# Merging triangular inverses of a gated delta rule: 64x64 tiles on the diagonal in place of 128x128 matmuls

## The chip, the cores and the metric

The kernel runs on one core of one Trainium2 chip. The metric is the device time of one execution in microseconds (us), the median of three runs. A core has a matmul engine (PE, with its weight loads shown apart as PEld), a vector engine (DVE), an activation engine (ACT), a general engine (POOL) and an engine that issues transfers (SP).

## The reference

The program is a decoder of two layers with attention, cross-attention and feed-forward parts. The change lies in the attention part of the second layer, a delta rule with gates. Per token t, for 16 sequences (B), 8 heads (H), 256 tokens, keys of 64 (DK) and values of 128 (DV):

```python
def step(carry, inp):
    ...
    s = s * alpha[..., None]
    u = jnp.einsum('bhd,bhdv->bhv', kt, s)
    s = s - beta[..., None] * jnp.einsum('bhd,bhv->bhdv', kt, u)
    s = s + beta[..., None] * jnp.einsum('bhd,bhv->bhdv', kt, vt)
    out = jnp.einsum('bhdv,bhd->bhv', s, qt)
```

The kernel doesn't step through the tokens. It forms for each tile of 128 tokens the lower triangular matrix of decayed products of keys and solves with its inverse: (I + L)^-1 applied to the values, and from that the outputs.

## The kernel before

The function is `delta_stage`, called once. The work is 32 "duos" (DUOS) of 2 units each (u = 0, 1). A unit is 2 heads h with 2 tiles s of 128 tokens, so it has TAU = 4 square matrices k of 128 x 128. Everything is fp32; a matmul in the program then shows in the trace as 2 weight loads and 2 matmul records.

`schedule` writes the order for every engine alike, and each engine runs its own instructions in that order:

```python
for m in range(DUOS + LATE):
    for slot in range(10):
        if LATE <= m:
            third(m - LATE, slot)
        if m < DUOS:
            first(m, slot)
        if 1 <= m <= DUOS:
            second(m - 1, slot)
            lanes(m - 1, slot)
```

So a round m works on three duos at once. There are 35 rounds of 10 slots. In words:

- `first` on PE: slot 0 scores the diagonal (L2930), and slots 1, 3, 5, 7, 9 score levels 0 to 4 (`level`, L2915), each as tiles of 64 rows x 128 columns of the array. DVE cuts the results into AB (L3081, L3092), and POOL multiplies the decays into `src` (L2899 once per unit after the diagonal, L2880 to L2890 after each level). Level 0 waits for both the decay (`decayed`) and the cut of the diagonal; level v waits for the scaling and the cut of level v - 1.
- `second`, one round later: level 5 in slot 2, level 6 in slot 6, the products between the two tiles in slot 8 (L2969). ACT cuts levels 5 and 6 (L3173, L3181) and scales `src` between them (L3159, L3162).
- `lanes` on DVE: the inverses of the 16 x 16 blocks, one lane per block, step by step. SP moves blocks out and in through DRAM: AB to l_img to lane_l, lane_x and lane_t to x_img and xt_img, and those as whole matrices to X and XT.
- `third`, three rounds later: slots 0 to 5 merge the 16 x 16 inverses to 32, to 64 and to 128. X holds the inverse, XT its transpose, LT is the triangle. Slot 0 forms y4 = LT'X (L2989), which DVE masks into Y4 (L3127). Slot 1 forms XT's and X's new blocks (L2997, L2999), which DVE subtracts (L3134, L3136). Slot 2 forms y5 (L3005), which ACT copies to Y5 (L3203). Slot 3 forms the new blocks (L3011, L3013); ACT writes XT (L3210), DVE X (L3141). Slot 4 forms y6 (L3019), ACT copies it to Y6 (L3215). Slot 5 forms XT's last block (L3025), ACT writes it (L3218). Slots 6 to 9 solve and make the outputs (L3033 to L3057).

Between the slots 4 and 5 of `third` no other PE work stands; between any two others stands a level, the diagonal or the cross product. Every merge matmul before uses all 128 rows and 128 columns of the array (weights 128 x 128), with 64 or 32 moving columns.

Of the kernel before, what the change touches and what calls it, by code (L numbers as in the profile page):

```python
# [21 lines left out]
P = 128  # L22
# [2617 lines left out]
def delta_stage(nc, name, ident, unit_in, unit_v, unit_o):  # L2640
# [27 lines left out]
    with Stage(nc, name) as st:  # L2668
# [17 lines left out]
        real = st.sb("real", [P, LOW + 1, P // 2])  # L2686
        keys_mask = st.sb("keys_mask", [P, LOW, 2, P // 2], I32)
# [54 lines left out]

        def rows_cols(k):
            h, s = divmod(k, 2)
            return slice(h * DK, (h + 1) * DK), slice(s * P, (s + 1) * P)
# [23 lines left out]
        with st.block() as block:  # L2769
            @block.sync  # L2770
            def _(sp):
                sp.wait_ge(zeroed, 1)
                for s in range(2):
                    sp.dma_start(whole(x_img, s), X[:, 0, :, :, :].rearrange("p u k t -> p (u k) t")).then_inc(img_zeroed, 16)
                    sp.dma_start(whole(xt_img, s), X[:, 0, :, :, :].rearrange("p u k t -> p (u k) t")).then_inc(img_zeroed, 16)
# [27 lines left out]
                def lanes_out(n):  # L2803

                    sp.wait_ge(lanes_done, n + 1)
                    if n < 2:
                        sp.wait_ge(img_zeroed, 64)
                    else:
                        sp.wait_ge(x_loaded[n % 2], 32 * (n // 2))
# [36 lines left out]
            def _(pool):  # L2846
                pool.memset(X[:, 0, :, :, :], 0.0).then_inc(zeroed, 1)
# [15 lines left out]
                pool.memset(Y5[:, :, :, :], 0.0).then_inc(zeroed, 1)  # L2863
                pool.memset(Y6[:, :, :, :], 0.0).then_inc(zeroed, 1)
# [42 lines left out]
            def _(pe):  # L2907
                pe.wait_ge(zeroed, 6)
                pe.wait_ge(masks_cast, 4)

                def level(n, v, u):
                    for k in (0, 2, 1, 3):
                        h, s = divmod(k, 2)
                        rows, cols = rows_cols(k)
                        ins = pe.matmul(lb[u][:, h, :, s * 64:(s + 1) * 64].rearrange("p a (b i) -> p a b i", i=1 << v),  # L2915
                                        src[rows, n % 3, u, 3, cols],
                                        halves(src[rows, n % 3, u, 0:2, cols], v)[:, :, :, 1, :], start=True, stop=True)
                    return ins
# [54 lines left out]
                def third(n, slot):  # L2973
                    w = n % 2
                    for u in range(2):
                        LT = lambda k: AB[:, n % KEPT, u, k // 2, 0, k % 2, :]
                        y = wp[u][:, :, :].rearrange("p k t -> p (k t)")[:, 0:256].rearrange("p (k t) -> p k t", k=TAU)
                        d = dp[u][:, :, :].rearrange("p k t -> p (k t)")
                        d1 = d[:, 0:256].rearrange("p (k t) -> p k t", k=TAU)
                        d2 = d[:, 256:512].rearrange("p (k t) -> p k t", k=TAU)  # L2980
                        if slot == 0:
                            if u == 0:
                                pe.wait_ge(x_loaded[w], 32 * (n // 2 + 1))
# [4 lines left out]
                            for k in range(TAU):  # L2988
                                ins = pe.matmul(y[:, k, :].rearrange("p (b i) -> p b i", i=16), LT(k),  # L2989
                                                halves(X[:, w, u, :, :], 4)[:, k, :, 0, :], start=True, stop=True)  # L2990
                            ins.then_inc(y4_scored, 1)
                        elif slot == 1:
# [3 lines left out]
                            for k in range(TAU):  # L2996
                                pe.matmul(d1[:, k, :].rearrange("p (b i) -> p b i", i=16), Y4[:, u, k, :],  # L2997
                                          halves(XT[:, w, u, :, :], 4)[:, k, :, 1, :], start=True, stop=True)
                                ins = pe.matmul(d2[:, k, :].rearrange("p (b i) -> p b i", i=16), XT[:, w, u, k, :],  # L2999
                                                halves(Y4[:, u, :, :], 4)[:, k, :, 0, :], start=True, stop=True)  # L3000
                            ins.then_inc(x4_scored, 1)
                        elif slot == 2:
                            pe.wait_ge(x4_ready, after(n, u))
                            for k in range(TAU):
                                ins = pe.matmul(y[:, k, :].rearrange("p (b i) -> p b i", i=32), LT(k),  # L3005
                                                halves(X[:, w, u, :, :], 5)[:, k, :, 0, :], start=True, stop=True)
                            ins.then_inc(y5_scored, 1)
                        elif slot == 3:
                            pe.wait_ge(y5_ready, after(n, u))
                            for k in range(TAU):  # L3010
                                pe.matmul(d1[:, k, :].rearrange("p (b i) -> p b i", i=32), Y5[:, u, k, :],  # L3011
                                          halves(XT[:, w, u, :, :], 5)[:, k, :, 1, :], start=True, stop=True)
                                ins = pe.matmul(wp[u][:, 2, k * 32:(k + 1) * 32], XT[:, w, u, k, :], Y5[:, u, k, 0:32],  # L3013
                                                start=True, stop=True)
                            ins.then_inc(x5_scored, 1)
                        elif slot == 4:
                            pe.wait_ge(x5_ready, after(n, u))
                            for k in range(TAU):
                                ins = pe.matmul(y[:, k, :], LT(k), X[:, w, u, k, 0:64], start=True, stop=True)  # L3019
                            ins.then_inc(y6_scored, 1)  # L3020
                        elif slot == 5:
                            pe.wait_ge(y6_ready, after(n, u))
                            pe.wait_ge(xt5_ready, after(n, u))
                            for k in range(TAU):
                                ins = pe.matmul(d1[:, k, :], Y6[:, u, k, :], XT[:, w, u, k, 64:128],  # L3025
# [37 lines left out]
            def _(dve):  # L3063
# [5 lines left out]
                dve.wait_ge(zeroed, 6)  # L3069
# [3 lines left out]
                dve.wait_ge(masks_cast, 4)  # L3073
# [44 lines left out]
                def third(n, slot):  # L3118
                    w = n % 2
                    for u in range(2):  # L3120
                        y = wp[u][:, :, :].rearrange("p k t -> p (k t)")[:, 0:256].rearrange("p (k t) -> p k t", k=TAU)
                        d = dp[u][:, :, :].rearrange("p k t -> p (k t)")
                        d1 = d[:, 0:256].rearrange("p (k t) -> p k t", k=TAU)
                        d2 = d[:, 256:512].rearrange("p (k t) -> p k t", k=TAU)
                        if slot == 0:
# [3 lines left out]
                                              real[:, LOW, :].rearrange("p (b i) -> p b i", i=16).unsqueeze(1)  # L3129
                                              .to_broadcast([P, TAU, 4, 16]), ALU.mult).then_inc(y4_ready, 1)  # L3130
                        elif slot == 1:
                            dve.wait_ge(x4_scored, after(n, u))
                            xt = halves(XT[:, w, u, :, :], 4)[:, :, :, 1, :]
                            dve.tensor_tensor(xt, xt, d1.rearrange("p k (b i) -> p k b i", i=16), ALU.subtract)  # L3134
# [3 lines left out]
                        elif slot == 3:  # L3138
                            dve.wait_ge(x5_scored, after(n, u))
                            x = X[:, w, u, :, 0:32]  # L3140
                            dve.tensor_tensor(x, x, wp[u][:, 2, :].rearrange("p (k j) -> p k j", k=TAU), ALU.subtract).then_inc(x5_ready, 1)  # L3141
# [7 lines left out]
            def _(act):  # L3149
# [44 lines left out]
                def third(n, slot):  # L3194
                    w = n % 2
                    for u in range(2):
                        y = wp[u][:, :, :].rearrange("p k t -> p (k t)")[:, 0:256].rearrange("p (k t) -> p k t", k=TAU)
                        d1 = dp[u][:, :, :].rearrange("p k t -> p (k t)")[:, 0:256].rearrange("p (k t) -> p k t", k=TAU)
                        if slot == 2:
                            act.wait_ge(y5_scored, after(n, u))  # L3200
                            for b in range(2):
                                rows = slice(b * 64 + 32, b * 64 + 64)
                                ins = act.activation(Y5[rows, u, :, b * 64:b * 64 + 32], y[rows, :, b * 32:b * 32 + 32],  # L3203
                                                     ACT.Copy)
                            ins.then_inc(y5_ready, 1)
                        elif slot == 3:
                            act.wait_ge(x5_scored, after(n, u))
                            for b in range(2):
                                rows = slice(b * 64, b * 64 + 32)
                                ins = act.activation(XT[rows, w, u, :, b * 64 + 32:b * 64 + 64],  # L3210
                                                     d1[rows, :, b * 32:b * 32 + 32], ACT.Copy, scale=-1.0)
                            ins.then_inc(xt5_ready, 1)
                        elif slot == 4:
                            act.wait_ge(y6_scored, after(n, u))
                            act.activation(Y6[64:128, u, :, 0:64], y[64:128, :, :], ACT.Copy).then_inc(y6_ready, 1)  # L3215
                        elif slot == 5:
                            act.wait_ge(xt6_scored, after(n, u))
                            act.activation(XT[0:64, w, u, :, 64:128], d1[0:64, :, :], ACT.Copy, scale=-1.0  # L3218
# [290 lines left out]
```

## Time and profile before

| | |
|---|---|
| median of 3 runs | 7280.35 us (7275.85 to 7287.11) |
| profiled execution | 7309.51 us, its span 7307.6 us |
| busy in the span | PE 5607.2, DVE 4967.0, ACT 3317.2, PEld 3111.2, POOL 2010.7 us |
| delta stage on PE | from 3910.4 to 5036 us |

The time is that of the whole program; the stage that is changed is about 1,126 us of it. PE's clock is granted at one of two levels, full (2.4 GHz) or half (1.2 GHz), shown as 1.00 or 0.50 of full speed; a value between is the mean of a stretch. A matmul's record begins when it enters the array and is pipelined with the next, so intervals between starts say more than the length of a record.

### The profile page before, as it was taken

How to read it: one execution, taken by the hardware profiler on the slowest of the kernel's cores; microseconds unless marked ns; L12 is line 12 of the kernel's file. 1: busy time of each engine (PE TensorE's matmuls, PEld its weight loads, DVE VectorE, ACT ScalarE, POOL GpSimd, SP SyncE). 2: the span in 40 equal slices, each digit the busy share in tenths (PEclk: the TensorE clock that was granted, in tenths of full speed). 3: DMA queues.
4: the chain of work that ended last, by engine and by line, in shares of the span. 5: the costliest groups of instructions: out<-in, count | busy, mean ns of one | idle time of the engine just before them, and what ended most of it. 6: DMA issues, size and time to landing. Idle time of an engine off the chain costs nothing. (4 is left out here: it accounts for less than half of the span.)

```text
span 7307.6 us, 135138 instructions
## 1 busy us (share of the span) xinstructions
PE 5607.2 (77%) x43987; PEld 3111.2 (43%) x43987; DVE 4967.0 (68%) x8964; ACT 3317.2 (45%) x4792; POOL 2010.7 (28%) x2592
## 2 busy tenths in 40 slices
PE   3786647688888839950787999997666699999759
PEld 1343435222222224420555999996534333333334
DVE  5564663799999944457896666663544599999654
ACT  0233424466666712220783444443223377777512
POOL 1101324566766720000004555551313200000000
PEclk6898878799999969975997999897787799999979
DMA  2220016222222210000233434342204422222200
GB/s 59 49 44 9 6 31 211 76 56 58 56 58 57 50 37 10 0 2 3 115 125 115 122 110 126 107 117 64 75 6 158 133 66 64 63 65 65 60 11 12
DMA packets 756225, 484.32 MB, mean 66 GB/s; under 512 B 484248, under 2 KB 682753, under 8 KB 754369
## 3 DMA queue, kind: packets, MB, share of 16 engines
q1 hardware_dynamic: 755904, 480.05, 23.2%
q8 instruction: 202, 3.31, 0.2%
q14 instruction: 119, 0.97, 0.0%
HBM read 282.34 MB, written 196.37 MB: 66 GB/s over the span
## 5 line engine op out<-in xcount | busy, mean ns | idle before, releaser
L1481 ACT ACTIVATE c0a_raised<-c0a_sb 128x1024 f32<-128x1024 f32 (+1 forms) x832 | 837.3, 1025 | 320.5 <-PE c0a_sb L1293 316.2
L1246 POOL TENSOR_SCALAR c0a_prob<-c0a_raised 128x1024 f32<-128x1024 f32 (+1 forms) x832 | 866.1, 1041 | 395.1 <-ACT c0a_raised L1481 363.5
L1481 ACT ACTIVATE c1a_prob<-c1a_sb 128x1024 f32<-128x1024 f32 (+1 forms) x832 | 828.9, 1029 | 205.6 <-PE c1a_sb L1293 202.0
L1369 DVE TENSOR_REDUCE c0a_pmax<-c0a_sa 128x2 f32<-128x802 f32 (+1 forms) x704 | 697.2, 990 | 86.3 <-PE c0a_sa L1261 81.9
L1369 DVE TENSOR_REDUCE c1a_pmax<-c1a_sa 128x2 f32<-128x802 f32 (+1 forms) x704 | 698.3, 992 | 70.7 <-PE c1a_sa L1261 66.7
L1261 PE MATMUL c0a_sa<-c0a_K,c0a_Q 48*128 48x401 bf16 (+1 forms) x2048 | 479.4, 354 | 196.8 <-DVE c0a_pmax L1369 101.5
L1261 PE MATMUL c1a_sa<-c1a_K,c1a_Q 48*128 48x401 bf16 (+1 forms) x2048 | 466.2, 346 | 103.4 <-DVE c1a_pmax L1369 47.7
L1312 PE MATMUL c0a_pv<-c0a_prob,c0a_V 128*9 128x256 f32 x6656 | 533.9, 392 | 4.8 <-POOL c0a_prob L1246 4.1
L1312 PE MATMUL c1a_pv<-c1a_prob,c1a_V 128*9 128x256 f32 x6656 | 519.4, 383 | 0.7 <-issue 0.5
L1261 PEld LDWEIGHTS c0a_sa<-c0a_K,c0a_Q 48*128 48x128 bf16 x2048 | 131.1, 94 | 688.6 <-DVE c0a_pmax L1369 330.9
L3092 DVE COPY_PREDICATED dd_AB<-dd_keys_mask,dd_lb 128x512 f32<-128x512 int32 x320 | 286.7, 959 | 156.2 <-PE dd_lb L2915 142.2
L1293 PE MATMUL c0a_sb<-c0a_Q,c0a_K 51*128 51x256 bf16 (+1 forms) x3328 | 384.1, 279 | 0.8 <-ACT c0a_raised L1481 0.8
L1293 PE MATMUL c1a_sb<-c1a_Q,c1a_K 51*128 51x256 bf16 (+1 forms) x3328 | 376.6, 272 | 0.9 <-ACT c1a_prob L1481 0.9
L1374 DVE TENSOR_REDUCE c0a_pmax<-c0a_sa 128x1 f32<-128x401 f32 (+1 forms) x640 | 361.5, 565 | 12.8 <-PE c0a_sa L1261 10.4
L1374 DVE TENSOR_REDUCE c1a_pmax<-c1a_sa 128x1 f32<-128x401 f32 (+1 forms) x640 | 362.8, 567 | 5.1 <-PE c1a_sa L1261 2.0
L1261 PEld LDWEIGHTS c1a_sa<-c1a_K,c1a_Q 48*128 48x128 bf16 x2048 | 127.6, 93 | 555.4 <-DVE c1a_pmax L1369 276.3
L2880 POOL TENSOR_TENSOR dd_src<-dd_src,dd_total 128x128 f32<-128x128 f32 x512 | 219.3, 450 | 395.4 <-PE dd_lb L2915 395.2
L1537 POOL TENSOR_TENSOR c1o_yn<-c1o_y,c1o_r 128x256 f32<-128x256 f32 x8 | 6.1, 782 | 1146.4 <-DMA c1o_r<-y_scale 1146.4
L2915 PE MATMUL dd_lb<-dd_src 64*128 64x128 f32 x3584 | 310.6, 319 | 10.1 <-POOL dd_total L2884 4.9
L2915 PEld LDWEIGHTS dd_lb<-dd_src 64*128 64x128 f32 x3584 | 260.3, 217 | 38.4 <-issue 9.2
L2538 PE MATMUL dp_qk<-d_HT,dp_wk 128*128 (+1 forms) x128 | 43.4, 421 | 284.5 <-DVE dp_bmat L2597 213.1
L930 DVE TENSOR_REDUCE s_pmax<-s_sa 128x2 f32<-128x512 f32 x256 | 170.5, 687 | 125.4 <-PE s_sa L822 123.1
(595 smaller groups left out, 12068.0 us busy)
## 6 DMA issues: line engine op xcount, KB each, us to landing
unit_in<-dp_res SPq DMA_DIRECT2D x64, 512.0 KB, 2.6
dd_src<-unit_in SPq DMA_DIRECT2D x64, 512.0 KB, 6.3
k_ctx<-c0k_parts SPq DMA_DIRECT2D x16, 1200.8 KB, 4.7
c0a_K<-k_ctx SPq DMA_DIRECT2D x128, 150.1 KB
k_ctx<-c1k_parts SPq DMA_DIRECT2D x16, 1200.8 KB, 4.7
c1a_K<-k_ctx SPq DMA_DIRECT2D x128, 150.1 KB
unit_v<-dp_vs SPq DMA_DIRECT2D x64, 256.0 KB, 2.8
dd_l_img<-dd_AB SPq DMA_DIRECT2D x64, 256.0 KB
```

The lines of the kernel that those rows point to most:

```text
L930: dve.tensor_reduce(pmax[:, u, 2 * h + tiles[0]:2 * h + tiles[0] + m, k:k + 1] .rearrange("p m a -> p (m a)"), sa[:, i % 2, 0:m * (b - a)] ...
L1246: pool.tensor_scalar(prob[0:r, in_ring(v, c), :, :, :], raised[0:r, in_ring(v, c), :, :, :], 1.0, math.exp(-FLOOR), ALU.min, ALU.max).then ...
L1261: return pe.matmul(tile[:, 0:b - a], Q[at, v, pr, s * P:(s + 1) * P], K[at, v, pr, a:b], start=True, stop=True)
L1293: ins = pe.matmul(sb_[0:r, in_both(v, c), e, pr, :], K[at, v, pr, c * P:c * P + r], Q[at, v, pr, :], start=True, stop=True)
L1312: ins = pe.matmul(pv[x * 32:x * 32 + V9, 0, :], V[0:r, v, c, x, :], prob[0:r, in_ring(v, c), x // 2, x % 2, :], start=(c == 0), stop=(c == ...
L1369: dve.tensor_reduce(pmax[:, u, :, 2 * pr + s, k], sa2[:, :, 0:w], AX.X, ALU.max).then_inc(a_reduced, 1)
L1374: dve.tensor_reduce(pmax[:, u, x % 2, 2 * pr + s, k:k + 1], sa1[:, 0:w], AX.X, ALU.max).then_inc(a_reduced, 1)
L1481: act.activation(dst[0:r, in_ring(v, c), :, :, :], sb_[0:r, in_both(v, c), :, :, :], ACT.Exp).then_inc(b_exp, 1)
L2538: pe.matmul(qk[:, u, 0, :], wk[:, rows], x, start=True, stop=True)
L2880: pool.tensor_tensor(kq[:, x], kq[:, x], tot[:, :, 0].unsqueeze(2).to_broadcast([P, nb, c]), ALU.mult)
L2915: ins = pe.matmul(lb[u][:, h, :, s * 64:(s + 1) * 64].rearrange("p a (b i) -> p a b i", i=1 << v), src[rows, n % 3, u, 3, cols], halves(sr ...
L3092: dve.copy_predicated(out[:, :, :, 1, :], mask.unsqueeze(1).to_broadcast([P, 4, P // c, c]), lb[u][:, :, :, 0:P].rearrange("p h a (b i) -> ...
```

## The change

Blocks of 16, 32 and 64 never cross the middle of the 128 x 128 matrix, so the merges are done on its two diagonal quarters:

- X is kept as the two diagonal blocks of 64 x 64, one under the other in [128, 64]. Y4 and Y6 halve to 64 columns, Y5 quarters to 32.
- Slots 0, 1 and 2 issue two matmuls (b = 0, 1) with weights of 64 x 64 and 32 moving columns for each old one of 128 x 128 with 64. The two use the array's quarters at rows and columns 0 to 63 and 64 to 127.
- Slot 3 issues for each k two matmuls with weights of 64 rows x 32 columns and one with 64 x 64, in turn.
- Slots 4 and 5 keep the number of matmuls; each uses one 64 x 64 quarter.
- Level 6 of `second` loads 64 columns of weights in place of 128.
- DVE: Y4 and X halve in elements; XT of slot 1 becomes two operations of 64 partitions; X of slot 3 is 32 partitions. A new pair_mask [128, 32] is made once at the start.
- ACT: Y5 is one operation of 128 x 128 in place of two of 32 x 128.
- SP: X is loaded by two transfers of 64 partitions in place of one, so each duo waits for 48 and not 32.
- At the start: two memsets of POOL (Y5, Y6) are gone, Y4's halves.

```diff
-        X = st.sb("X", [P, 2, 2, TAU, P])
-        Y4 = st.sb("Y4", [P, 2, TAU, P])
-        Y5 = st.sb("Y5", [P, 2, TAU, P])
-        Y6 = st.sb("Y6", [P, 2, TAU, P])
+        X = st.sb("X", [P, 2, 2, TAU, P // 2])
+        Y4 = st.sb("Y4", [P, 2, TAU, P // 2])
+        Y5 = st.sb("Y5", [P, 2, TAU, P // 4])
+        Y6 = st.sb("Y6", [P, 2, TAU, P // 2])
...
+        def half(b):
+
+            return slice(b * 64, (b + 1) * 64)
...
-                    sp.dma_start(X[:, n % 2, :, :, :].rearrange("p u k t -> p (u k) t"), whole(x_img, n % 2)
-                                 ).then_inc(x_loaded[n % 2], 16)
+                    for b in range(2):
+                        sp.dma_start(X[half(b), n % 2, :, :, :].rearrange("p u k t -> p (u k) t"),
+                                     whole(x_img, n % 2)[half(b), :, half(b)]).then_inc(x_loaded[n % 2], 16)
...
                 def level(n, v, u):
+                    keys = 64 if v == 6 else P
...
-                                        src[rows, n % 3, u, 3, cols],
+                                        src[rows, n % 3, u, 3, s * P:s * P + keys],
...
                         if slot == 0:
...
                             for k in range(TAU):
-                                ins = pe.matmul(y[:, k, :].rearrange("p (b i) -> p b i", i=16), LT(k),
-                                                halves(X[:, w, u, :, :], 4)[:, k, :, 0, :], start=True, stop=True)
+                                for b in range(2):
+                                    ins = pe.matmul(y[half(b), k, :].rearrange("p (b i) -> p b i", i=16),
+                                                    LT(k, half(b), half(b)),
+                                                    halves(X[half(b), w, u, :, :], 4)[:, k, :, 0, :],
+                                                    start=True, stop=True)
...
                         elif slot == 3:
                             pe.wait_ge(y5_ready, after(n, u))
                             for k in range(TAU):
-                                pe.matmul(d1[:, k, :].rearrange("p (b i) -> p b i", i=32), Y5[:, u, k, :],
-                                          halves(XT[:, w, u, :, :], 5)[:, k, :, 1, :], start=True, stop=True)
-                                ins = pe.matmul(wp[u][:, 2, k * 32:(k + 1) * 32], XT[:, w, u, k, :], Y5[:, u, k, 0:32],
-                                                start=True, stop=True)
+                                for b in range(2):
+                                    pe.matmul(d1[b * 64:b * 64 + 32, k, :], Y5[half(b), u, k, :],
+                                              XT[half(b), w, u, k, b * 64 + 32:b * 64 + 64], start=True, stop=True)
+                                ins = pe.matmul(wp[u][0:64, 2, k * 32:(k + 1) * 32], XT[0:64, w, u, k, 0:64],
+                                                Y5[0:64, u, k, :], start=True, stop=True)
                             ins.then_inc(x5_scored, 1)
                         elif slot == 4:
                             pe.wait_ge(x5_ready, after(n, u))
                             for k in range(TAU):
-                                ins = pe.matmul(y[:, k, :], LT(k), X[:, w, u, k, 0:64], start=True, stop=True)
+                                ins = pe.matmul(y6[64:128, k, :], LT(k, half(0), half(1)), X[0:64, w, u, k, :],
+                                                start=True, stop=True)
```

How PE's instructions stand before, from slot 0 of a round to the level of slot 3; each row is a line, what it writes and reads, the partitions x free size of the result, and how many in a row:

```order
-L2989 MATMUL dd_wp<-dd_X,dd_AB 128x64 x8
-L2930 MATMUL dd_lb<-dd_src 128x128 x8
-L2997 MATMUL dd_dp<-dd_XT,dd_Y 128x64
-L2999 MATMUL dd_dp<-dd_Y,dd_XT 128x64
...
-L2915 MATMUL dd_lb<-dd_src 128x2x64 x8
-L3005 MATMUL dd_wp<-dd_X,dd_AB 128x64 x8
-L2915 MATMUL dd_lb<-dd_src 128x2x64 x8
-L3011 MATMUL dd_dp<-dd_XT,dd_Y 128x64
-L3013 MATMUL dd_wp<-dd_Y,dd_XT 128x32
...
-L3019 MATMUL dd_wp<-dd_X,dd_AB 128x64 x8
-L3025 MATMUL dd_dp<-dd_XT,dd_Y 128x64 x8
```

The pairs of lines 2997 and 2999, and of 3011 and 3013, come 8 times each. The same place with the change, whose lines have moved down by 9 to 21:

```order
+L3000 MATMUL dd_wp<-dd_X,dd_AB 64x32 x16
+L2940 MATMUL dd_lb<-dd_src 128x128 x8
+L3011 MATMUL dd_dp<-dd_XT,dd_Y 64x32 x2
+L3015 MATMUL dd_dp<-dd_Y,dd_XT 64x32 x2
...
+L2924 MATMUL dd_lb<-dd_src 128x2x64 x8
+L3024 MATMUL dd_wp<-dd_X,dd_AB 64x32 x16
+L2924 MATMUL dd_lb<-dd_src 128x2x64 x8
+L3031 MATMUL dd_dp<-dd_XT,dd_Y 32x32 x2
+L3033 MATMUL dd_wp<-dd_Y,dd_XT 64x32
...
+L3039 MATMUL dd_wp<-dd_X,dd_AB 64x64 x8
+L3046 MATMUL dd_dp<-dd_XT,dd_Y 64x64 x8
```

No instruction has moved past another; the merges' matmuls of a round have gone from 64 to 104, and in slot 3 a pair with 32 result partitions and a single one with 64 now stand in turn, 8 times.

DVE in slot 1, before and with the change (one unit after the other):

```order
-L3134 TENSOR_TENSOR dd_XT<-dd_XT,dd_dp 128x16x16
-L3136 TENSOR_TENSOR dd_X<-dd_X,dd_dp 128x16x16
-L3134 TENSOR_TENSOR dd_XT<-dd_XT,dd_dp 128x16x16
-L3136 TENSOR_TENSOR dd_X<-dd_X,dd_dp 128x16x16
...
+L3157 TENSOR_TENSOR dd_XT<-dd_XT,dd_dp 64x4x2x16 x2
+L3160 TENSOR_TENSOR dd_X<-dd_X,dd_dp 128x8x16
+L3157 TENSOR_TENSOR dd_XT<-dd_XT,dd_dp 64x4x2x16 x2
+L3160 TENSOR_TENSOR dd_X<-dd_X,dd_dp 128x8x16
```

DVE has one operation more per unit here, and the elements of each partition that X's takes are half.

## Rows read from the trace of the kernel before

**Rows 1.** Busy time by engine in three stretches of the delta stage.
```profile
core 0: us, PE busy (x) PEld busy (x) DVE busy (x) ACT busy (x) POOL busy (x), PEclk, DMA share, GB/s
3910.40:3977.10 66.70, 51.09 (x384) 41.03 (x384) 49.42 (x98) 15.39 (x48) 53.20 (x128) 0.61 0.29 84
3977.10:4926.90 949.80, 949.80 (x8751) 885.03 (x8752) 620.02 (x1487) 391.39 (x1176) 511.81 (x1237) 0.91 0.40 116
4926.90:5036.00 109.10, 107.99 (x856) 102.97 (x852) 40.41 (x112) 40.54 (x120) 18.34 (x45) 0.86 0.25 68
```

**Rows 2.** DVE's groups, 3977.10 to 4926.90 us: busy us, mean ns, idle before.
```profile
L3092 DVE COPY_PREDICATED dd_AB<-dd_keys_mask,dd_lb 128x512 f32<-128x512 int32 x281 | 251.0, 960 | 135.7 <-PE dd_lb L2915 126.7 <-DMA dd_l_img<-dd_AB 7.3
L3081 DVE COPY_PREDICATED dd_AB<-dd_eye_mask,dd_lb 128x512 f32<-128x512 int32 x56 | 37.9, 732 | 8.4 <-PE dd_lb L2930 8.4
```

**Rows 3.** Waits, 3982 to 4960 us: waited for in total, times, longest.
```profile
POOL dd_src L2880 <- PE dd_lb L2915: 449.4, 144, 5.9
ACT dd_Y L3203 <- PE dd_wp L3005: 282.3, 58, 9.8
PEld dd_dp L3053 <- issue: 9.6, 29, 0.3
```

**Rows 4.** Busy time in two neighbouring stretches of different clock, columns as in Rows 1.
```profile
4430.40:4444.00 13.60, 13.60 (x80) 12.81 (x80) 7.40 (x19) 5.60 (x20) 6.13 (x16) 0.50 0.01 2
4444.00:4498.60 54.60, 54.60 (x550) 50.74 (x548) 36.68 (x89) 22.33 (x65) 30.35 (x72) 1.00 0.50 144
```

**Rows 5.** PE in order of time at full clock, slots 3 to 5: start, length, records.
```profile
4395.51 0.43 PE L3011 MATMUL dd_dp<-dd_XT,dd_Y 128*128 128x64 f32 x2
...
4399.20 1.18 PE L2915 MATMUL dd_lb<-dd_src 64*128 64x128 f32 x16
4400.31 2.00 PE L3019 MATMUL dd_wp<-dd_X,dd_AB 128*128 128x64 f32 x16
...
4404.03 1.16 PE L2915 MATMUL dd_lb<-dd_src 64*128 64x128 f32 x16
```

**Rows 6.** PE in order of time, the next round's slot 8 to slot 3.
```profile
4410.57 1.14 PE L2969 MATMUL dd_lb<-dd_src 64*128 64x256 f32 x8
4411.63 0.49 PE L3053 MATMUL dd_dp<-dd_W,dd_AB 128*128 128x128 f32 x2
...
4415.60 2.00 PE L2989 MATMUL dd_wp<-dd_X,dd_AB 128*128 128x64 f32 x16
4417.53 1.16 PE L2930 MATMUL dd_lb<-dd_src 64*128 64x128 f32 x16
4418.62 0.43 PE L2997 MATMUL dd_dp<-dd_XT,dd_Y 128*128 128x64 f32 x2
...
4422.33 1.18 PE L2915 MATMUL dd_lb<-dd_src 64*128 64x128 f32 x16
4423.45 2.00 PE L3005 MATMUL dd_wp<-dd_X,dd_AB 128*128 128x64 f32 x16
```

**Rows 7.** Weight loads by shape: rows*columns, busy us, mean ns.
```profile
L2989 PEld LDWEIGHTS dd_wp<-dd_X,dd_AB 128*128 128x128 f32 x512 | 59.6, 191 | 3.6
L859 PEld LDWEIGHTS s_pv<-s_prob,s_VG 128*32 128x32 f32 x1024 | 20.3, 108 | 45.4 <-issue 20.4 <-DVE s_osb L981 12.8 <-ACT s_prob L1075 12.1
```

**Rows 8.** Busy time inside one level's matmuls, columns as in Rows 1.
```profile
4404.10:4404.84 0.74, 0.74 (x14) 0.74 (x16) 0.05 (x1) 0.72 (x3) 0.01 (x1) 1.00 0.00 0
```

**Rows 9.** POOL in order of time, the decay of one round.
```profile
4418.37 2.51 POOL L2899 TENSOR_TENSOR dd_src<-dd_src 128x512 f32<-128x512 f32 x2
```

**Rows 10.** ACT in order of time around slot 4.
```profile
4399.88 0.82 ACT L3159 ACTIVATE dd_src<-dd_src,dd_total 128x64 f32<-128x64 f32 x3
4400.61 0.73 ACT L3162 ACTIVATE dd_src<-dd_src,dd_total 128x32 f32<-128x32 f32 x3
4401.45 0.38 ACT L3215 ACTIVATE dd_Y<-dd_wp 64x256 f32<-64x256 f32 x1
```

**Rows 11.** POOL in order of time at the stage's start.
```profile
3907.56 0.95 POOL L2863 MEMSET dd_Y<- 128x1024 f32 x1
3908.45 1.23 POOL L2864 MEMSET dd_Y<- 128x1024 f32 x1
```

More of the change, by code:

```diff
@@ L2686, in delta_stage @@
         real = st.sb("real", [P, LOW + 1, P // 2])
+        pair_mask = st.sb("pair_mask", [P, P // 4])
         keys_mask = st.sb("keys_mask", [P, LOW, 2, P // 2], I32)
@@ L2996, in third @@
                             for k in range(TAU):
[L2997 to L3000, printed above, removed]
+                                for b in range(2):
+                                    pe.matmul(d1[half(b), k, :].rearrange("p (b i) -> p b i", i=16), Y4[half(b), u, k, :],
+                                              halves(XT[half(b), w, u, :, half(b)], 4)[:, k, :, 1, :],
+                                              start=True, stop=True)
+                                for b in range(2):
+                                    ins = pe.matmul(d2[half(b), k, :].rearrange("p (b i) -> p b i", i=16),
+                                                    XT[half(b), w, u, k, half(b)],
+                                                    halves(Y4[half(b), u, :, :], 4)[:, k, :, 0, :],
+                                                    start=True, stop=True)
                             ins.then_inc(x4_scored, 1)
@@ L3004, in third @@
                             for k in range(TAU):
-                                ins = pe.matmul(y[:, k, :].rearrange("p (b i) -> p b i", i=32), LT(k),
-                                                halves(X[:, w, u, :, :], 5)[:, k, :, 0, :], start=True, stop=True)
+                                for b in range(2):
+                                    ins = pe.matmul(y[half(b), k, :], LT(k, half(b), half(b)), X[half(b), w, u, k, 0:32],
+                                                    start=True, stop=True)
                             ins.then_inc(y5_scored, 1)
@@ L3068, in _ @@
                                 ident[:, :].unsqueeze(1).to_broadcast([P, TAU, P])).then_inc(masks_cast, 1)
-                dve.wait_ge(zeroed, 6)
+                dve.tensor_tensor(pair_mask[:, :], real[:, LOW, 0:P // 4], real[:, LOW, P // 4:P // 2], ALU.add
+                                  ).then_inc(masks_cast, 1)
+                dve.wait_ge(zeroed, 4)
                 for s in range(2):
@@ L3128, in third @@
                                               y.rearrange("p k (b i) -> p k b i", i=16),
-                                              real[:, LOW, :].rearrange("p (b i) -> p b i", i=16).unsqueeze(1)
-                                              .to_broadcast([P, TAU, 4, 16]), ALU.mult).then_inc(y4_ready, 1)
+                                              pair_mask[:, :].rearrange("p (b i) -> p b i", i=16).unsqueeze(1)
+                                              .to_broadcast([P, TAU, 2, 16]), ALU.mult).then_inc(y4_ready, 1)
                         elif slot == 1:
                             dve.wait_ge(x4_scored, after(n, u))
-                            xt = halves(XT[:, w, u, :, :], 4)[:, :, :, 1, :]
-                            dve.tensor_tensor(xt, xt, d1.rearrange("p k (b i) -> p k b i", i=16), ALU.subtract)
+                            for b in range(2):
+                                xt = halves(XT[half(b), w, u, :, half(b)], 4)[:, :, :, 1, :]
+                                dve.tensor_tensor(xt, xt, d1[half(b), :, :].rearrange("p k (b i) -> p k b i", i=16),
+                                                  ALU.subtract)
                             x = halves(X[:, w, u, :, :], 4)[:, :, :, 0, :]
```

67 lines of the change are left out of this document (33 added, 34 removed).

## The prediction

> **What bounds the kernel now.** I read first the busy time by stretch, since the change touches one stage only. In its long middle stretch of 949.80 us PE is busy for all 949.80 us, DVE for 620.02, POOL for 511.81 and ACT for 391.39 [rows 1]. The diagonal's cut runs twice a round and 56 times there [rows 2], so the stretch is 28 rounds and a round takes 33.92 us; of that DVE is busy for 22.1, POOL for 18.3 and ACT for 14.0. The list of waits says the same from the other side: POOL and ACT wait for PE's results for hundreds of us, and what PE itself waited for is some 10 us of issue [rows 3]. So PE bounds the stage; what its order and its clock cost is what the change can give back.
>
> Two things hide in a "busy" PE. One is the clock. There are 8751 / 28 = 312.5 matmul records a round [rows 1]; at full clock 550 records take 54.60 us, 0.0993 us each, and at half clock 80 take 13.60 [rows 4]. A round at full clock would thus take 31.0 us, and the stage pays 2.9 us a round for stretches at half clock. The other is what a matmul costs. In slots 4 and 5, 32 records go in 3.72 us (4400.31 to 4404.03), and slot 1's 32 records in 3.71 (4418.62 to 4422.33) [rows 5, 6]. That is 0.112 us a record, whether 64 or, in slot 3 (4395.51 to 4399.20, 3.69 us), in part 32 columns stream. So the matmul's moving side doesn't set the price, the load of 128 weight columns does. Levels, whose weights have 64 rows on either half of the array, give 14 records in 0.74 us, 0.053 each [rows 8]: two loads go beside each other. Slots 0 to 5 of the merges cost before 1.93 + 3.71 + 1.93 + 3.69 + 3.72 = 15.0 us a round [rows 5, 6] (slot 2 is like slot 0).
>
> **The change, part by part.**
>
> Price of a record on a quarter. No row has a load of 64 fp32 columns. A load record of 128 columns lasts 191 ns, one of 32 lasts 108 [rows 7]: linear between them, 64 columns last 136. I take the step between starts to be proportional to columns, 0.112 x 64/128 = 0.056 us; the bounds are 0.028 (that of 32 columns, were only moving columns to count) and 0.112 (nothing gained). Two quarters with their own rows and columns I take to run beside each other, as the levels' halves do.
>
> Price of a change of tile size. Slot 0's step is 1.93 us with 16 x 0.112 = 1.79 in it, 0.14 over; a level is 1.09 to 1.11 us with 16 x 0.053 = 0.85 in it, 0.25 over [rows 5, 6]. The mean is 0.19 us a change, about 0.1 of which is the first weight load that nothing hides; with 64 columns that part halves, so 0.13 us. Bounds are 0 and 0.19.
>
> The slots then are, at full clock: slot 0, 32 records in pairs, 16 x 0.056 + 0.13 = 1.0; slot 1, 64 records, 1.9; slot 2, 1.0; slots 4 and 5, 32 records on one quarter one after the other, 1.8 + 0.13 = 1.9. Slot 3 has 8 groups. In each the two 32-column matmuls go beside each other and the 64-column one behind them: 2 x 0.03 + 2 x 0.056 = 0.17 us, 1.4 together. But 64x32 and 64x64 stand in turn, so the tile size changes 16 times more: 16 x 0.13 = 2.1, together 3.5 us (from 1.4 + 0.13 without a price on the turn to 1.4 + 16 x 0.19 = 4.4). The sum is 9.3 in place of 15.0: 5.7 us less a round, a round of 25.3 us at full clock.
>
> The Trainium skill, page "TensorEngine Tiling (Array Packing)", Key Properties, states that a change of tiling mode drains TensorE, and this speaks against slot 3. The trace agrees that a change costs something: 0.25 us over at a level. By the page slot 3 pays in all 16 changes, which is what my sum takes; without it the round would be 23.3 us.
>
> Level 6. Half the weight columns, but 128 moving columns stay. The cross product streams 256 columns in 8 records in 1.06 us (4410.57 to the next at 4411.63) [rows 6]: less 0.2 for the change, 0.107 a record with pairs beside each other, 0.213 each for 256 columns. So 128 columns are 0.107 each for themselves, and nothing is gained. Bound: 0 to 0.4 us.
>
> What is late next. As PE's slots shrink, two waits show that PE now covers.
> First, level 0 in slot 1 waits for POOL's decay of both units, which ends at 4418.37 + 2.51 = 4420.88, 5.3 us after slot 0 began at 4415.60 [rows 6, 9]. POOL starts it behind the last scaling of the round before, so it doesn't move. PE would be at level 0 after 1.0 + 1.1 + 1.9 = 4.0 us: up to 1.3 us of wait, less half a level since unit 0 may start first. I take 1.0. Behind PE queue slots 2 and 3, and nobody else is late.
> Second, slot 5 waits for ACT's Y6 with no level between. Before, ACT first ran the scaling of level 5 up to 4401.34 and then Y6 at 4401.45, 1.1 us after slot 4 began, while PE had 1.8 us of slot 4 to do [rows 5, 10]. Slot 4 now takes 0.9 us, so PE stands at slot 5 after 1.0, while unit 0's Y6 is ready at some 1.6 and unit 1's 0.38 later. I take 0.8 (0.5 to 1.2).
> DVE has 22 us of work a round, its slot 1 grows by one operation a unit and slots 0 and 1 lose elements: about even. It keeps under PE's 27. So a round at full clock is 25.3 + 1.8 = 27.1 us. SP's third transfer a duo lies rounds ahead of its use: nothing.
>
> The clock. The half-clock stretch shown begins at 4430.40 [rows 4], where slot 3 of its round ends (slot 2 begins at 4423.45, slot 3 some 3 us later [rows 6]); there the array streams the fewest columns. Such a stretch of 13.6 us loses 6.8, so 2.9 us a round is one in 2.3 rounds. The stretches of slow feeding become shorter in slots 0 to 2, but slot 3 stays a weak one and the two waits add gaps. I can't derive this; between 0 and the 2.9 us of now I take 1.2. A round: **28.3 us**, 5.6 less than 33.9.
>
> The sum. 28 rounds and the one from 4926.90 on: 29 x 5.6 = 163 us. The last three rounds have merges and no levels; of the 109.10 us from there 75 are theirs [rows 1], and each loses its merges' 5: 15. The start: two memsets of POOL, 0.89 + 1.2 us, stand ahead of PE's first matmul [rows 11]; DVE has a mask more to make there; I take 1.2 us (0 to 2.2). Together 179. The profiled execution took 7309.51 us, so 7130 for one like it, which lies 29.2 above the median of the runs; against the median **7101 us**.
>
> **The rivals.**
>
> B: the turn of sizes in slot 3 is free. If a 64x32 matmul and a 64x64 one follow each other without a drain, slot 3 is 1.5 us, the round 25.1 with its waits and 26.2 with clock: 29 x 7.7 + 16 = 240, **7040 us**. For it: the price 0.19 was seen only between work of different shapes with a wait on a semaphore at the boundary. Against it: from L2915 to L3019 0.25 us is paid, and the list of waits has no such wait of PE [rows 3, 5].
>
> C: a record has a least price of its own. Then 64 columns cost no less than the best rate seen, and 208 records (104 matmuls) stand where 128 stood. Nothing in the program goes faster than the 0.053 us a record of the levels [rows 8], so the trace can't exclude that this is a floor. With 0.053 the merges are 11.0 + 1.2 of the changes of before + 2.1 = 14.3, a gain of 0.7; the case decides for slower from 0.056 on. At 0.068, a level's 1.09 us over its 16 records, it is 14.1 (its change within) + 2.1 = 16.2, 1.2 us more a round: 32 x 1.2 less 1, **7320 us**, and with 0.053 it is 7257. Against it: two levels' records go in pairs, so the issue isn't what spaces them.
> The Trainium skill, "TensorE: Matmul & The Clock Gate", Wait — 56ns, not 53.3ns?, gives about 62 ns per MATMUL where hardware decode is off, and 25 ns otherwise. By the first this case comes out, with an estimate of 208 x 0.062 + 3.3 = 16.2 us for the merges; the 0.053 of the trace speaks for the second.
>
> D: the clock stays low. If thinner feeding keeps PE at half clock for a share h of the time, the round is 25.3 / (1 - h/2), the waits gone. Break-even is h = 0.51; now it is 2 x 2.9 / 33.9 = 0.17. For h = 0.6 it is 36.1 us and the time **7345**. For it: the first three rounds, which have no merges and in which PE is busy for 51 of 66.7 us, ran at a mean of 0.61 [rows 1]. Against it: the merges' quarters still stream in nearly all of the time.
>
> E: another engine sets the pace. Cuts of 0.96 us [rows 2] stand twice between two levels, and DVE does the merges' own steps first; with each slot only 2 to 3 us long, some end late, and 27.1 becomes 30.5 with no further cost of clock: 29 x 3.4 + 16 = 115, **7166 us**.
>
> **How the numbers follow.** I give my forecast 0.5, B 0.16, C 0.16, D 0.08, E 0.10. The likeliest is 7101 us; its own range, from the bounds of slot 3 (±1 us), waits (±0.5) and clock (±1.2), is 7055 to 7150. The range takes in B's 7040 with its bounds and E, from 7015 to 7225; beyond it are most of C and D and a rest of B. What a measurement can tell from no change is 0.2%, 15 us. Faster: A, B, E and a part of C, 0.80; within 0.2%: 0.06 from C; slower: 0.14 from C and D.
>
> **What would show it.** In order of time at full clock: slot 0 about 1.0 us from its first merge record to the diagonal's, slot 1 1.9, slots 4 and 5 together 1.9 and a gap between them ahead of which ACT's Y6 stands; slot 3 3.5 us (1.5 would be B, over 4.4 a drain dearer than seen). Ahead of level 0 PE idles about 1 us behind POOL's L2899, now a later line. If the intervals between records on quarters are 0.053 or more even in pairs, it is C. The mean clock of the middle stretch is to be at or above 0.93; under 0.75 it is D. A round with DVE busy at over 0.9 is E. The forecast is wrong if quarters' weight loads don't run beside each other, since slots 0 to 2 then save nothing.

## The result and the profile after

The changed kernel takes 7201.78 us (7196.43 to 7213.07, 4 runs), the one before 7283.73 (4 runs): a ratio of 0.9894 (0.9878 to 0.9909), some 82 us faster. I had forecast 7101 and 179 us. The time is within the stated range of 7015 to 7225; the gain is less than half of the 179 us.

The profiled execution has a span of 7211.4 us. Two stretches of the delta stage, the 28 full rounds and the tail, that answer to [rows 1] (busy us and records by engine, then the clock):

```profile
core 0: us, PE busy (x) PEld busy (x) DVE busy (x) ACT busy (x) POOL busy (x), PEclk, DMA share, GB/s
3956.66:4846.96 890.30, 861.62 (x10978) 761.35 (x10980) 634.57 (x1543) 376.12 (x1120) 508.87 (x1231) 0.82 0.40 115
4846.96:4945.00 98.04, 94.61 (x1168) 85.06 (x1168) 41.53 (x121) 38.05 (x111) 19.74 (x50) 0.74 0.27 74
```

A round takes 31.8 us (890.30 / 28) where it took 33.9. PE now idles for 28.7 us in all, 1.0 a round, and its mean clock has gone from 0.91 to 0.82. The stage as a whole (3889.95 to 4945.00) went from 1126 to 1055 us, some 70 less: 59 in the full rounds, 11 in the tail, nothing in the first three rounds (66.7 us in both). The two profiled spans differ by 96 us, since the stage also starts 20 us earlier. That part isn't the change: in the profile of b_wide3 below, which alters nothing ahead of slot 3, the full rounds begin at 3952.38, 25 us earlier than before too.

PE in order of time, which answers to [rows 5, 6] (start, length, records; in brackets how long PE sat idle before, and what ended it):

```profile
4401.43 1.12 PE L3000 MATMUL dd_wp<-dd_X,dd_AB 64*64 64x32 f32 x32
4402.48 1.16 PE L2940 MATMUL dd_lb<-dd_src 64*128 64x128 f32 x16
4403.57 0.30 PE L3011 MATMUL dd_dp<-dd_XT,dd_Y 64*64 64x32 f32 x4
...
4405.55 0.72 PE L2924 MATMUL dd_lb<-dd_src 64*128 64x128 f32 x8
4406.76 0.72 PE L2924 MATMUL dd_lb<-dd_src 64*128 64x128 f32 x8 [0.48 <-POOL dd_src L2907]
4407.41 1.12 PE L3024 MATMUL dd_wp<-dd_X,dd_AB 64*64 64x32 f32 x32
4408.64 0.71 PE L2924 MATMUL dd_lb<-dd_src 64*128 64x128 f32 x8
4409.80 0.72 PE L2924 MATMUL dd_lb<-dd_src 64*128 64x128 f32 x8 [0.45 <-DVE dd_AB L3115]
4410.45 0.25 PE L3031 MATMUL dd_dp<-dd_XT,dd_Y 64*32 64x32 f32 x4
4410.63 0.30 PE L3033 MATMUL dd_wp<-dd_Y,dd_XT 64*64 64x32 f32 x2
4410.86 0.25 PE L3031 MATMUL dd_dp<-dd_XT,dd_Y 64*32 64x32 f32 x4
...
4414.06 2.08 PE L2924 MATMUL dd_lb<-dd_src 64*128 64x128 f32 x16
4416.06 1.86 PE L3039 MATMUL dd_wp<-dd_X,dd_AB 64*64 64x64 f32 x15
```

The slots did shrink: slot 0 is 1.05 us (4401.43 to 4402.48), slot 1 1.98, a group of slot 3 0.41 (4410.45 to 4410.86). Level 0 waits for POOL's decay, level 5 (the next two rows of L2924) for a cut of DVE. But the 16 records of L2924 from 4414.06 last 2.08 us, where the 16 of L2940 at 4402.48 last 1.16: the clock has halved. Three neighbouring stretches of the same round, to be held against [rows 4]:

```profile
4402.00:4412.90 10.90, 9.87 (x200) 8.49 (x196) 8.86 (x24) 2.59 (x8) 8.11 (x18) 1.00 0.67 184
4412.90:4423.10 10.20, 10.20 (x85) 9.37 (x84) 6.25 (x15) 5.16 (x19) 5.37 (x14) 0.51 0.28 103
4423.10:4444.00 20.90, 19.87 (x309) 17.28 (x308) 16.34 (x41) 8.18 (x22) 12.81 (x31) 0.99 0.40 93
```

The clock falls between 1.5 and 3.4 us after slot 3's first record, and slot 3 takes 3.28 us. Half-clock stretches now come 28 times in 28 rounds and last 317 us together. Before they came 13 times, 178 us, each 3.8 to 4.1 us after slot 3's first record, so just behind its 3.69 us. No round of the changed kernel is free of them, so its full-clock round is an estimate: 26.2 us, the full-clock round of the grouped kernel below, and the 1.38 that slot 3 is longer here give 27.6. The kernel with wider streams, also below, gives the same: its full-clock rounds take 28.2 us, 0.62 of which slot 3 is longer there. So the clock costs 4.2 us a round. That is where most of the expected gain went.

### The profile page after: what moved, and what is told of

The parts are those of the page before. It is cut to its first block and busy times, and to the rows that moved or that the text cites. A ratio compares the mean times of both kernels' runs of the same rounds, so it can differ in the third digit from the quotient of the medians.

```text
span 7211.4 us, 140243 instructions
## 1 busy us (share of the span) xinstructions
PE 5480.0 (76%) x46501; PEld 2956.1 (41%) x46547; DVE 4981.5 (69%) x9029; ACT 3299.7 (46%) x4728; POOL 2005.8 (28%) x2590
## 5 line engine op out<-in xcount | busy, mean ns | idle before, releaser
L1369 DVE TENSOR_REDUCE c1a_pmax<-c1a_sa 128x2 f32<-128x802 f32 (+1 forms) x704 | 698.1, 992 | 70.7 <-PE c1a_sa L1261 66.7
L2924 PE MATMUL dd_lb<-dd_src 64*128 64x128 f32 (+1 forms) x3584 | 359.3, 347 | 39.0 <-POOL dd_src L2907 15.9
L2924 PEld LDWEIGHTS dd_lb<-dd_src 64*128 64x128 f32 (+1 forms) x3584 | 292.8, 230 | 79.6 <-issue 28.5
```

The lines of the kernel that those rows point to most:

```text
L1369: dve.tensor_reduce(pmax[:, u, :, 2 * pr + s, k], sa2[:, :, 0:w], AX.X, ALU.max).then_inc(a_reduced, 1)
L2924: ins = pe.matmul(lb[u][0:keys, h, :, s * 64:(s + 1) * 64] .rearrange("p a (b i) -> p a b i", i=1 << v), src[rows, n % 3, u, 3, s * P:s * ...
```

## The experiments

Each ratio is to runs of the kernel before on the same chip (medians 7274 to 7284 us); two variants are best compared by their ratios. Full-clock rounds are medians of the rounds without a half-clock stretch. Theory 1: the clock falls where the array is fed with few columns, and slot 3, thin and with sixteen changes of tile size, is the place. Theory 2: it goes by how much of the array is in use, so quarter tiles lower it whatever streams. Beside them, rivals for the waits.

**Before, slot 3 with wider streams.**

```diff
-    pe.matmul(d1[:, k, :].rearrange("p (b i) -> p b i", i=32), Y5[:, u, k, :],
-              halves(XT[:, w, u, :, :], 5)[:, k, :, 1, :], start=True, stop=True)
-    ins = pe.matmul(wp[u][:, 2, k * 32:(k + 1) * 32], XT[:, w, u, k, :], Y5[:, u, k, 0:32],
-                    start=True, stop=True)
+    pe.matmul(dp[u][:, k, :], Y5[:, u, k, :], XT[:, w, u, k, :], start=True, stop=True)
+    ins = pe.matmul(wp[u][:, 2 + k // 2, k % 2 * 64:k % 2 * 64 + 64], XT[:, w, u, k, :],
+                    Y5[:, u, k, 0:64], start=True, stop=True)
```

DVE and ACT read the same elements from their new places.

> The kernel before with one thing changed: slot 3 streams more columns through the same weights (128 in place of 64 for the transposed block, 64 in place of 32 for the other); the results that are used are the same. Theory 1 (the half-clock stretch comes where the array is fed with few columns per time): slot 3 keeps its 3.7 us, since 128 weight columns bound it, the stretches of half clock after it go, a round falls from 34.0 to 31.0 us, the mean clock of the stage rises from 0.91 to near 1.00 and the program is 80 to 90 us faster (about 7195). Theory 2 (the clock has to do with something else, such as the small tiles of the levels or the waits of the other engines): no change within 15 us.

Measured: 7185.8 us, ratio 0.9885 (0.9861 to 0.991). The 28 rounds, in the columns of [rows 1], and slot 3 in order of time:

```profile
3952.38:4820.38 868.00, 868.00 (x8746) 807.11 (x8748) 626.78 (x1487) 389.52 (x1176) 510.20 (x1235) 1.00 0.44 127
```
```profile
4394.94 0.49 PE L3011 MATMUL dd_dp<-dd_XT,dd_Y 128*128 128x128 f32 x2
4395.27 0.33 PE L3012 MATMUL dd_wp<-dd_Y,dd_XT 128*128 128x64 f32 x2
...
4398.66 1.18 PE L2915 MATMUL dd_lb<-dd_src 64*128 64x128 f32 x16
```

Slot 3 lasts 3.72 us as before (3.69 in [rows 5]), with the same instructions and twice the columns, and no half-clock stretch is left: 31.0 us a round, the number that [rows 1, 4] give for full clock. Theory 1 is shown for the kernel before: with all else equal, the columns of slot 3 decide whether the clock falls. It is also a gain of 88 us, as much as the whole change brought.

**After, slot 3 all of 64x32 tiles.**

```diff
-    ins = pe.matmul(wp[u][0:64, 2, k * 32:(k + 1) * 32], XT[0:64, w, u, k, 0:64],
+    ins = pe.matmul(wp[u][32:64, 2, k * 32:(k + 1) * 32], XT[0:64, w, u, k, 32:64],
```

> The changed kernel with slot 3 all of one tile size: the matmul with weights 64x64 uses only the 32 columns whose results are read, so all 24 matmuls are 64x32 and the 16 changes of size inside slot 3 are gone. If a change of size drains the array at about 0.13 us, slot 3 falls from 3.3 to about 1.5 us at full clock. Theory 1 (thin feeding sets off the half clock): also the low stretch of each round gets rarer, as slot 3 was the thinnest place: a round from 31.9 to between 25.5 and 29, the program 7040 to 7140 us. Theory 2 (the clock goes by how much of the array is in use): the low stretch stays in each round, a round 30.2, 7145 to 7155 us. If turns are free: no change.

Measured: 7055.35 us, ratio 0.9708 (0.9683 to 0.9733).

```profile
3950.40:4706.40 756.00, 697.21 (x10978) 618.28 (x10978) 632.10 (x1541) 372.71 (x1120) 508.52 (x1231) 0.94 0.47 135
```
```profile
4390.30 0.22 PE L3031 MATMUL dd_dp<-dd_XT,dd_Y 64*32 64x32 f32 x2
...
4390.93 1.18 PE L2924 MATMUL dd_lb<-dd_src 64*128 64x128 f32 x16
4392.04 1.14 PE L3039 MATMUL dd_wp<-dd_X,dd_AB 64*64 64x64 f32 x16
4394.25 1.14 PE L3046 MATMUL dd_dp<-dd_XT,dd_Y 64*64 64x64 f32 x16 [1.07 <-ACT dd_Y L3235]
```

A round is 27.0 us, 25.6 at full clock. Slot 3 is 0.63 us from its first record at 4390.30 to the level, shorter than I thought possible, and PE hits the next wait: 1.07 us for ACT's Y6 ahead of slot 5. Low stretches still come 22 times, but short, 88 us in all. They begin 4.4 to 5.9 us after slot 3's first record, so no longer in slot 3 but behind this wait (slot 5 begins 3.95 us after it).

**After, slot 3 grouped.**

```diff
     for k in range(TAU):
         for b in range(2):
             pe.matmul(d1[b * 64:b * 64 + 32, k, :], ...
+    for k in range(TAU):
         ins = pe.matmul(wp[u][0:64, 2, ...
```

> The changed kernel with the order inside slot 3 changed: for a unit first the eight 64x32 matmuls, then the four 64x64 ones, so 4 changes of size a round inside slot 3 in place of 16; same matmuls. With a price of about 0.13 us a change slot 3 goes from 3.3 to 1.8 us at full clock; if changes are free it stays. The clock may stay as low as it is; 7130 to 7160 us if it does, less if the low stretch gets rarer.

Measured: 7053.78 us, ratio 0.9697 (0.967 to 0.9724).

```profile
3970.28:4711.48 741.20, 704.01 (x10972) 621.68 (x10972) 622.48 (x1541) 372.80 (x1120) 505.15 (x1230) 0.99 0.48 138
```
```profile
4405.10 0.44 PE L3031 MATMUL dd_dp<-dd_XT,dd_Y 64*32 64x32 f32 x16
4405.47 0.65 PE L3034 MATMUL dd_wp<-dd_Y,dd_XT 64*64 64x32 f32 x8
4406.05 0.44 PE L3031 MATMUL dd_dp<-dd_XT,dd_Y 64*32 64x32 f32 x16
4406.42 0.65 PE L3034 MATMUL dd_wp<-dd_Y,dd_XT 64*64 64x32 f32 x8
4407.00 1.18 PE L2924 MATMUL dd_lb<-dd_src 64*128 64x128 f32 x16
```

The same matmuls in another order: slot 3 at full clock is 1.90 us (4405.10 to 4407.00) where it was 3.28 (8 groups of 0.41) with twelve changes of size more, 0.115 us a change. And the clock falls in 2 rounds where it fell in all 28, though the tiles, the columns and the two waits ahead of slot 3 (0.47 and 0.44 us, 0.48 and 0.45 in the changed kernel) are the same. This rules out theory 2, that quarter tiles lower the clock whatever streams. It also sharpens theory 1: the number of columns is the same too, and what is shorter is the time that they are spread over. The sum is 5.3 us a round, of which 1.4 is slot 3 itself and some 3.9 the clock.

**After, wider streams in slots 0 to 3.** Each 32 moving columns become 64, e.g.

```diff
-    ins = pe.matmul(y[half(b), k, :], LT(k, half(b), half(b)), X[half(b), w, u, k, 0:32],
+    ins = pe.matmul(y6[half(b), k, :], LT(k, half(b), half(b)), X[half(b), w, u, k, :],
```

> The changed kernel with 64 moving columns in place of 32 in every merge matmul of slots 0 to 3 (in slot 3's single matmul the same 32 columns twice); the extra results are not read. Weights and tile sizes as in the changed kernel. Theory 1 (feeding): PE's slots 0 to 2 keep their length within 0.1 us, the half-clock stretch of each round gets shorter or rarer, a round falls from 31.9 to 27 to 30 us and the program is at 7060 to 7150 us. Theory 2 (share of the array in use): no change, 7200, or slower by what the columns cost, up to 1 us a round (7230).

Measured: 7167.71 us, ratio 0.9856 (0.9831 to 0.9881).

```profile
3968.85:4807.95 839.10, 806.20 (x10972) 687.48 (x10974) 627.20 (x1540) 374.69 (x1120) 507.21 (x1231) 0.92 0.42 122
```

30.0 us a round and 11 low stretches in place of 28. The streams cost 0.03 us in slot 0, but slot 3 goes from 3.28 to 3.90. I take the reason to be that a 32-column weight load doesn't hide 64 moving columns; nothing tests it by itself. I had left that out of the forecast, and the time lies above my 7060 to 7150 for theory 1, though below the 7200 of theory 2.

**After, level 6 with 128 weight columns again,** on the grouped kernel:

```diff
-    keys = 64 if v == 6 else P
+    keys = P
```

> The kernel with slot 3 grouped, and level 6 with 128 weight columns as before the change. Its 128 moving columns bound it either way, so I expect no change: 7054 us within 10.

Measured: 7059.89 us, ratio 0.9689 (0.9663 to 0.9714); the grouped kernel's 0.9697 (0.967 to 0.9724) doesn't differ. Rounds at full clock are 26.3 us against 26.2. This part of the change brings at most 0.1 us a round.

**Grouped, POOL's last scaling of unit 1 behind the decay.**

```diff
-                        for u in range(2):
+                        for u in range(1 if slot == 9 else 2):
                             scale(n, LEVEL_AT[slot], u)
...
+                def second(n, slot):
+                    if slot == 0:
+                        scale(n, LOW - 1, 1)
```

> The kernel with slot 3 grouped, and on POOL the last scaling (level 4) of unit 1 behind the decay of the next duo in place of ahead of it. In a round at full clock PE waits 0.75 us behind level 0, 0.2 in front of and 0.7 us behind level 5. If all of these start from the late decay (level 0 late, so its cuts late, so level 5 late), a round goes from 26.2 to 24.7 to 25.3 us and the program from 7054 to 7015 to 7035. If DVE's cuts hold level 5 by themselves only the first wait goes, and the others grow by as much: 7050 to 7055.

Measured: 7131.11 us, ratio 0.9788 (0.9763 to 0.9813), against 0.9697 for the grouped kernel: some 66 us slower than that, and outside both of my ranges. DVE and, under it, PE in order of time in one round:

```profile
4391.61 1.25 DVE L3139 TENSOR_TENSOR dd_lane_p<-dd_lane_x,dd_lane_l 64x1 f32<-64x1 f32 x1
4392.90 0.14 DVE L3143 TENSOR_REDUCE dd_lane_x<-dd_lane_p 64x1 f32<-64x1 f32 x1
4392.97 0.58 DVE L3162 TENSOR_TENSOR dd_XT<-dd_XT,dd_dp 64x128 f32<-64x128 f32 x2
...
4394.36 0.29 DVE L3165 TENSOR_TENSOR dd_X<-dd_X,dd_dp 128x128 f32<-128x128 f32 x1
4394.56 2.48 DVE L3120 COPY_PREDICATED dd_AB<-dd_keys_mask,dd_lb 128x512 f32<-128x512 int32 x2
```
```profile
4392.62 1.18 PE L2928 MATMUL dd_lb<-dd_src 64*128 64x128 f32 x16
4393.90 1.45 PE L3028 MATMUL dd_wp<-dd_X,dd_AB 64*64 64x32 f32 x32
4396.03 0.72 PE L2928 MATMUL dd_lb<-dd_src 64*128 64x128 f32 x8 [0.68 <-DVE dd_AB L3120]
4397.19 1.23 PE L2928 MATMUL dd_lb<-dd_src 64*128 64x128 f32 x8 [0.45 <-DVE dd_AB L3120]
```

My chain of causes was wrong, and of the rival the part on the waits held: level 0 no longer waits (16 records in one piece), but DVE isn't free before 4394.56, since the merges' own steps stand ahead of the cuts. All that PE gained it loses in front of level 5, where slot 2's start and level 5's are 2.13 us apart in place of 1.24. A full-clock round is 26.5 where it was 26.2. What neither of my ranges had is the clock: it falls 15 times in place of 2, and a round is 29.0 on the mean. In 11 of the 15 it falls 1.4 to 1.7 us ahead of slot 3's first record, as here at 4396.70, right behind the gap and before slot 3 has begun:

```profile
4394.56:4396.70 2.14, 1.33 (x24) 1.10 (x24) 2.14 (x3) 0.55 (x2) 2.14 (x6) 0.99 0.01 1
4396.70:4398.35 1.65, 1.20 (x11) 0.97 (x9) 1.44 (x8) 0.75 (x2) 1.22 (x3) 0.50 0.51 116
```

The matmuls are the same and PE idles for about as long (1.5 us a round for 1.3). So the idle time's place matters, and slot 3 isn't needed ahead of a fall; that the one longer gap is the cause is my reading, from this step alone.

**All 64x32, ACT's scaling of level 5 one slot later.**

```diff
-                    if slot in (3, 4):
-                        scale_high(n, 5, slot - 3)
+                    if slot in (4, 5):
+                        scale_high(n, 5, slot - 4)
```

> The kernel with slot 3 all of 64x32 tiles, and ACT's scaling of level 5 one slot later for each unit (slots 4 and 5 in place of 3 and 4), so that it stands behind the copies of Y6 and of XT. If PE's wait ahead of slot 5 is the price of ACT's order, the step from slot 4 to slot 5 falls from 2.21 to 1.2 us and a round at full clock from 25.6 to 24.6; with fewer gaps the clock should also fall less often: 7005 to 7030 us. If the wait is that of PE's result on its way to ACT and back: 7050 to 7060. If level 6 then waits for the scaling in slot 6, up to 1 us of it is given back.

Measured: 6997.38 us, ratio 0.9611 (0.9585 to 0.9636), the fastest of all.

```profile
3944.82:4645.22 700.40, 670.26 (x10964) 585.77 (x10966) 622.84 (x1541) 365.37 (x1120) 505.63 (x1229) 1.00 0.51 146
```
```profile
4405.05 1.14 PE L3039 MATMUL dd_wp<-dd_X,dd_AB 64*64 64x64 f32 x16
4406.19 1.14 PE L3046 MATMUL dd_dp<-dd_XT,dd_Y 64*64 64x64 f32 x16
4407.26 1.67 PE L2924 MATMUL dd_lb<-dd_src 64*128 64x128 f32 x16
```

The wait ahead of slot 5 is gone, so it was ACT's order. Of the 1.07 us some 0.5 come back: the level behind slot 5 takes 1.60 us (4407.26 to the next work at 4408.86), 1.1 elsewhere. 25.0 us a round, no low stretch in the 28 rounds, somewhat better than the 7005 to 7030 that I expected.

**All 64x32 with wide streams,** without and with the step of ACT:

> The kernel with slot 3 all of 64x32 tiles, and 64 moving columns in every merge matmul of slots 0 to 3 as well. With 64x32 tiles alone a round was 25.6 us when the clock stayed full and 27.2 or 28.7 when it fell, mean 27.1. If thin feeding is what sets off the half clock, the wider streams keep nearly all rounds at full clock and a round is 25.7 to 26.3 us: 7015 to 7035 us. If what matters is that PE waits for ACT between slots 4 and 5 (1.3 us there now), the low stretches stay: 7050 to 7060. If columns cost time in slot 3 (they may: weights of 32 columns load fast), slot 3 goes from 0.63 to 1.1 us.

> The kernel with slot 3 all of 64x32 tiles and ACT's scaling one slot later, and the 64 moving columns in slots 0 to 3 as well. The version without the wide streams already ran nearly all rounds at full clock at 25.0 us. If the clock is all that the wider streams help, they now cost what they add to slot 3 (1.02 for 0.63 us), unless PE would have waited there anyway: a round of 25.0 to 25.4 us, 6995 to 7010 us. If they still lift the clock in the first and last rounds, up to 5 us less.

Measured: 7023.53 us, ratio 0.965 (0.9623 to 0.9676), and 7015.94 us, ratio 0.9648 (0.9625 to 0.9671).

```profile
3943.89:4663.39 719.50, 674.10 (x10976) 594.55 (x10976) 630.25 (x1542) 372.26 (x1120) 507.43 (x1231) 1.00 0.50 142
3949.71:4661.01 711.30, 683.53 (x10976) 595.08 (x10976) 623.26 (x1541) 364.86 (x1120) 505.84 (x1230) 1.00 0.50 144
```

The first bears theory 1 out again: with the waits still there, wider streams alone take 22 low stretches down to 2 short ones, 27.0 to 25.7 us. The step of ACT did the same with the narrow streams still there. So in this kernel it takes both, the thin streams and the wait ahead of slot 5, and removing either is all but enough. In the second nothing is left to lift, and the longer slot 3 costs 0.4 us a round (25.4), somewhat more than I said in time (7016 for 6995 to 7010).

## Why the prediction was wrong

- **What bounds the kernel**: right. PE did, and its round fell with its slots.
- **Price of a record on a quarter, and pairs beside each other**: right. Slots 0 and 1 were 1.05 and 1.98 us for forecasts of 1.0 and 1.9; slots 4 and 5 are 1.14 and 1.07 us in the fastest kernel (4405.05 to 4406.19 to 4407.26), 2.2 for a forecast of 1.9, which is 0.3 too low. Rival C, a floor of 0.053 us a record, is out: slot 0 has 32 records in 1.05 us, 0.033 each.
- **Changes of tile size in slot 3**: right. 0.115 us a change for 0.13, slot 3 3.28 us for 3.5. Rival B is out. The Trainium skill ("TensorEngine Tiling (Array Packing)", Key Properties) states that a change of tiling mode drains TensorE; the 0.115 us that a change costs here agrees.
- **Waits**: right in sum, and only half in place. POOL's decay costs 0.75 us (1.0 forecast). ACT's Y6 costs 0.4 with slot 3 grouped and 1.07 with it short (0.8 forecast); in the changed kernel itself it doesn't show, since slot 4 runs at half clock in every round. I had not foreseen DVE's cut of level 0, which holds level 5 back by 0.2 us in front of it and 0.7 between its two units, a part of rival E. A round at full clock is some 27.6 us, I said 27.1.
- **Level 6**: nothing, as forecast.
- **The clock**: this step failed. "Between 0 and the 2.9 us of now I take 1.2", and it is 4.2. With 31.8 for 28.3 us a round, 29 rounds miss 101 us. Of the 3.5 us, 3.0 are the clock. That 7202 less 7101 is also 101 is in part luck: the tail and the start miss a further 7 us or so, and the medians differ by some 12 more than the stage does.
- That the time still lies within the range is no merit of the clock's term: its upper bound of 2.9 was passed, 7202 lies outside the forecast's own range of 7055 to 7150, and the stated one is wider for the rivals' sake.
- What was wrong in the working: I took the present loss as the upper bound, as if a shorter slot could only feed the array better. I had rows for slot 3 as the place. The change put sixteen more drains into it and into no other slot, left only 32 moving columns in it, and set two new gaps ahead of it, and yet I kept the bound. The same rows gave the scale: a low stretch in each round in place of one in 2.3 costs 2.3 times as much, 6.7 us in the kernel before. Rival D had the mechanism, with h = 0.36 (317 of 890 us), between the 0.17 of before and the 0.51 of break-even, and its formula gives 30.8 us a round for that, near the 31.8; I had priced it only beyond the point where it turns the sign, and gave it 0.08.

What stays open: I didn't measure slot 3's turns with the waits of slots 1 and 2 taken away, so how the loss of clock divides between drains, thin columns and idle time is known only from single steps (grouping: 3.9 us; columns: 1.8 us of the mean round though slot 3 grew by 0.6). Whether a drain lowers the clock by anything but the time that it takes, no run tells. DVE's order in slot 1 wasn't tried.

## What to carry to other kernels

When a PE-bound kernel has half-clock stretches, look at what stands just ahead of them: matmuls bound by their weight load can stream more columns for next to nothing (3.69 to 3.72 us for slot 3 with 128 weight columns, though 3.28 to 3.90 once it has weights of 32), and doing so in one slot here was worth 88 us alone. When a change makes matmuls smaller, group those of one tile size, and price the clock as something that can get worse than it is, up to a fall in every round. A gap taken out at one place may come back at another and cost there more than its length: here it came back whole, and the round grew by 0.3 us at full clock and by 2.5 on the mean.

## What was not expected of the hardware

- Three 64x32 tiles run beside one another with their loads: slot 3 in that form has 48 records in 0.63 us, 0.013 us each, in place of 0.112 us for a record with 128 weight columns. The three tiles' records begin within 0.03 us of one another:

```profile
4390.77 0.20 PE L3031 MATMUL dd_dp<-dd_XT,dd_Y 64*32 64x32 f32 x2
4390.78 0.19 PE L3033 MATMUL dd_wp<-dd_Y,dd_XT 64*32 64x32 f32 x1
4390.80 0.20 PE L3031 MATMUL dd_dp<-dd_XT,dd_Y 64*32 64x32 f32 x2
```

- DVE's operation on one element per partition (L3139 above) took 1.25 us while POOL's decay ran, and ended at 4392.86, when the decay did (4390.35 + 2.50). In 27 of that profile's 28 full rounds the operation took over 0.8 us and ended within 0.02 us of the end of one of the decay's two operations. This speaks for DVE waiting for POOL there, though no run without POOL was made. It stands just ahead of the merges' steps and the cuts, so it adds to their delay. The pair of cuts took 2.48 us with POOL at work, where two of the mean length of [rows 2] are 1.9; for this POOL as the cause was not tested.
